# Loading x by halves of the lanes instead of by halves of its rows, in a DMA-fed graph layer on one core

## The chip, the core and the metric

The kernel runs on one core of a Trainium2 chip. The metric is the device time in microseconds (us) of one execution. It was run three times before the change, and once more with the profiler on.

## What is computed

With N = 5000 nodes and F = 64 features, the reference is:

```python
h = jnp.maximum(_layernorm(x, axis=-1), 0.0)
neighbors = adj_matrix @ h                      # 5000 x 5000 by 5000 x 64, float32
neighbors = neighbors / (num_neighbors[:, None] + 1e-07)
out = jnp.concatenate([h, neighbors], axis=-1) @ fc_w.T + fc_b
x = x + jax.nn.relu(out)
```

Nearly all bytes are those of the 5000 x 5000 float32 matrix adj, 100 MB, each of which is read once.

## The kernel before

**Layout.** A core's fast memory has 128 lanes. The first 4,608 nodes of x lie as 36 rows on each of the 128 lanes (lane p holds nodes 36p to 36p + 35), so that one lane's share is 36 x 64 x 4 = 9,216 contiguous bytes in the chip's main memory. The other 392 nodes lie as 4 rows on 98 lanes. adj comes in six column groups; each group is read in loads of up to four row tiles, the largest of which are 5,120 KB, 128 lanes x 40,960 bytes.

**Queues.** All loads of adj (33 of them) are issued by SyncE (SP), in a written order, into a ring in the tile `raw`, which holds three of the largest loads. A load whose place is still in use waits for `load_used`, the semaphore that TensorE raises when it has multiplied the load that lay there. The x of the first 4,608 nodes is loaded by `load_x(engine, k)`, called once on SP's queue with k = 0, ahead of every adj load, and once on ScalarE's (ACT's) queue with k = 1. Behind it ACT's queue issues the layer's weights fc_t (into the tile shown as `rnn_diag`), the bias, and the last 392 nodes of x. In the trace, q1 holds what SP issues and q10 what ACT issues.

**Order of the work.** `normalize(b)` on VectorE (DVE) works on five sets of eight tiles of x and waits first for both halves of x (`x_loaded[0]` at 32, 16 from each half). Its product, `h_pairs`, is transposed by TensorE (`turn`, L589), copied by ScalarE (L360), and multiplied with the weights (`weigh`, L601) into `g_sb`, which needs the weights to have landed and to have been doubled (L695). Only then do the multiplications with adj begin (`multiply`, L641). Sets 1 to 4 are normalized, turned and weighed between the multiplications of the first group. At the end each finished bank is scaled, turned back, and added to x; the result leaves in two stores.

Of the kernel before, what the change touches and what calls it, by code (L numbers as in the profile page):

```python
# [12 lines left out]
LANES = 128  # L13
# [31 lines left out]
def gnn_layer(nc, x, adj_groups, num_neighbors, fc_t, fc_b, out):  # L45
# [16 lines left out]
    TAIL0 = FULL * BLOCK  # L62
    REM0 = CH * LANES
    ROWS = FULL * RUN
# [59 lines left out]
    with ExitStack() as ctx:  # L124
        def sb(name, shape, dt=F32):
            return ctx.enter_context(nc.sbuf_tensor(name, shape, dt))
# [6 lines left out]
        x_sb = sb("x_sb", [LANES, TILES, F])  # L133
# [76 lines left out]
        def flat(v):  # L210
            return v.rearrange("p t f -> p (t f)")
# [41 lines left out]
            return landed[n % LANDINGS], 16 * (n // LANDINGS) + 16  # L253

        def load_x(engine, k):
            r = slice(ROWS // 2 * k, ROWS // 2 * (k + 1))
            engine.dma_start(x_sb[:, r, :], x[0:TAIL0, :].rearrange("(p r) f -> p r f", r=ROWS)[:, r, :]
                             ).then_inc(x_loaded[0], 16)

        def sync_program(sp):  # L260
            def load(n):
                g, m, i0, i1 = LOADS[n]
                w = WIDTH[g]
                if loads_before(n):
                    sp.wait_ge(load_used, loads_before(n))
                r = RUN if m < FULL else TAIL_RUN
                rows = adj_groups[g][m * BLOCK:m * BLOCK + r * LANES, 0:w].rearrange("(p i) c -> p (i c)", i=r)
                sp.dma_start(raw[:, place(n):place_end(n)], rows[:, i0 * w:i1 * w]).then_inc(loaded(n)[0], 16)

            load_x(sp, 0)  # L270
            for n in range(len(LOADS)):
                load(n)

            sp.wait_ge(out_ready, LAST)
            sp.dma_start(out[0:TAIL0, :].rearrange("(p r) f -> p (r f)", r=ROWS), flat(out_sb[:, 0:ROWS, :])
                         ).then_inc(stored, 16)
            sp.wait_ge(stored, 16)
# [40 lines left out]
        def scalar_program(act):  # L318
            def load_few():

                load_x(act, 1)
                act.dma_start(w_rows.rearrange("r (k c) -> r k c", k=2), fc_t.rearrange("(k r) c -> r k c", k=2)
                              ).then_inc(weights_loaded, 16)
                act.wait_ge(bias_cleared, 1)
                act.dma_start(bias_row[0:1, :], fc_b.rearrange("(a f) -> a f", a=1)).then_inc(bias_loaded, 16)
                act.dma_start(tail(x_sb)[0:PAD0], tail_nodes(x)[0:PAD0]).then_inc(x_loaded[1], 16)
                act.wait_ge(x_cleared, 1)
                act.dma_start(tail(x_sb)[PAD0:LAST_LANES], tail_nodes(x)[PAD0:LAST_LANES]).then_inc(x_loaded[1], 16)  # L330
# [431 lines left out]
```

## Time and profile before

| what | us |
|---|---|
| median of three runs | 246.04 |
| lowest, highest | 245.55, 246.4 |
| the profiled execution's own time | 246.15 |
| its span in the profile | 244.7 |
| TensorE (PE) busy | 201.6 |
| VectorE (DVE) busy | 41.7 |
| ScalarE (ACT) busy | 15.8 |

The span covers the program's instructions; 246.15 - 244.7 = 1.45 us of the profiled execution lie around it. The mean granted clock of TensorE was 0.993 of full. In the profile, a packet is one contiguous piece moved by one of the 16 DMA engines, and a share of busy time of "the 16 engines" is a mean over them. A packet is put into the stretch in which it ends, so a short stretch can show a share above 1 or none.

### The profile page before, as it was taken

The numbers are of one execution on the slowest core, as the hardware profiler recorded it, in microseconds if no ns is written. First come the engines' busy times: TensorE is split into PE (matmuls) and PEld (weight loads), VectorE is DVE, ScalarE is ACT, GpSimd is POOL, SyncE is SP. The second block draws the span as 40 slices with busy tenths as digits, with TensorE's granted clock in tenths as the row PEclk, the third lists the DMA queues.
The fourth block names the chain that finished last, engine by engine and source line by source line (L and its number), as shares of the span: only waits on it lengthen the run. The fifth ranks groups of instructions, "written<-read, shape, count | busy, mean of one in ns | idle before, by whom it ended". The sixth has DMA issues, their size and how long they took to land.

```text
span 244.7 us, 2442 instructions
## 1 busy us (share of the span) xinstructions
PE 201.6 (82%) x1090; PEld 85.9 (35%) x1090; DVE 41.7 (17%) x102; ACT 15.8 (6%) x36; POOL 6.1 (2%) x17
## 2 busy tenths in 40 slices
PE   0016899999879987997799897969899687996995
PEld 0014445435323433442343242424244232332354
DVE  1623404314400200050000530203000000000052
ACT  2102121201200110010000300000000000000000
POOL 6000010000000000000010000000000000000000
PEclk9999999999979999999999999999999999999999
DMA  8999999999999999999999999999999999999996
GB/s 300 431 431 438 435 429 410 426 429 429 426 442 442 429 425 429 429 429 408 425 435 428 460 424 434 408 460 424 440 408 459 404 445 399 429 429 412 414 393 254
DMA packets 5983, 102.76 MB, mean 420 GB/s; under 512 B 1122, under 2 KB 1710, under 8 KB 2902
## 3 DMA queue, kind: packets, MB, share of 16 engines
q1 hardware_dynamic: 5040, 101.61, 97.4%
q10 hardware_dynamic: 774, 0.84, 1.0%
q8 instruction: 8, 0.13, 0.2%
q0 software_dynamic: 160, 0.16, 0.2%
q14 instruction: 1, 0.01, 0.0%
HBM read 101.33 MB, written 1.28 MB: 419 GB/s over the span
## 4 chain that ended last, share of the span: by engine, by line
DMA 53%; PE 32%; issue 11%; DVE 2%; ACT 0%; ACTq 0%; DVEq 0%
DMA raw<-adj_group 46%; PE acc L641 24%; DMA rnn_diag<-fc_t 8%; PE turned L641 3%; PE y L601 3%; DVE rnn_diag L487 1%; PE y L626 1%; PE turned L589 0%; PE y L695 0%; PE y L618 0%; ACT g_sb L366 0%; PE y L669 0%; ACT w_both L387 0%; DVE out_sb L550 0%; DVE rnn_diag L495 0%
## 5 line engine op out<-in xcount | busy, mean ns | idle before, releaser
L641 PE MATMUL acc<-raw,g_sb 128*64 128x512 f32 (+1 forms) x780 | 160.3, 557 | 20.3 <-DMA raw<-adj_group 19.6
L641 PEld LDWEIGHTS acc<-raw,g_sb 128*64 128x64 f32 x780 | 55.2, 137 | 107.0 <-issue 75.2
L641 PE MATMUL turned<-raw,g_sb 128*64 128x196 f32 x156 | 18.2, 337 | 0.1
L641 PEld LDWEIGHTS turned<-raw,g_sb 128*64 128x64 f32 x156 | 11.4, 136 | 14.7 <-issue 13.7
L589 PE MATMUL turned<-ident,h_pairs 128*128 128x128 f32 x20 | 3.7, 315 | 12.4 <-DVE h_pairs L446 12.4
L516 DVE TENSOR_TENSOR sums<-acc,rnn_bc 128x512 f32<-128x512 f32 x4 | 2.7, 689 | 64.9 <-PE acc L641 63.0
L458 DVE TENSOR_TENSOR out_sb<-y,bias 128x128 f32<-128x128 f32 x20 | 4.4, 284 | 48.7 <-ACT g_sb L366 48.6
L601 PE MATMUL y<-w_both,ht 128*128 128x256 f32 (+1 forms) x40 | 11.9, 437 | 0.7 <-ACT w_both L387 0.7
L601 PEld LDWEIGHTS y<-w_both,ht 128*128 128x128 f32 x40 | 8.0, 217 | 3.9 <-issue 1.5
L434 DVE TENSOR_REDUCE var<-sums 128x8 f32<-128x512 f32 x5 | 3.4, 686 | 24.2 <-ACT sums L341 24.2
L542 DVE TENSOR_TENSOR out_sb<-y,out_sb 128x512 f32<-128x512 f32 (+1 forms) x5 | 3.2, 636 | 24.8 <-PE y L669 20.9
L589 PEld LDWEIGHTS turned<-ident,h_pairs 128*128 128x128 f32 x20 | 2.4, 156 | 13.9 <-issue 13.9
L366 ACT ACTIVATE g_sb<-y 128x256 f32<-128x256 f32 x10 | 3.3, 381 | 49.3 <-PE y L601 30.8
L695 PE MATMUL y<-rnn_diag,ident 64*64 64x128 f32 x4 | 0.7, 444 | 6.3 <-DMA rnn_diag<-fc_t 6.3
L487 DVE TENSOR_TENSOR rnn_diag<-ident,rnn 128x512 f32<-128x512 f32 x8 | 5.1, 687 | 0.2 <-PE y L626 0.2
L626 PE MATMUL y<-rnn_diag,ones 128*64 128x512 f32 (+1 forms) x20 | 4.6, 552 | 0.5 <-DVE rnn_diag L487 0.4
L371 ACT ACTIVATE rnn_bc<-y 128x512 f32<-128x512 f32 (+1 forms) x5 | 2.9, 588 | 31.7 <-PE y L626 31.7
L492 DVE TENSOR_TENSOR rnn_diag<-ident_twice,rnn 128x256 f32<-128x256 f32 x1 | 0.4, 426 | 25.7 <-issue 25.7
L423 DVE TENSOR_REDUCE mean<-x_sb 128x8 f32<-128x512 f32 (+1 forms) x6 | 3.5, 589 | 5.7 <-DMA x_sb<-x 5.7
L360 ACT ACTIVATE ht<-turned 128x512 f32<-128x512 f32 x5 | 3.0, 597 | 21.0 <-PE turned L589 21.0
L656 PE MATMUL acc<-adj_rem,g_sb 128*64 128x512 f32 (+1 forms) x20 | 4.2, 549 | 0.0
L430 DVE TENSOR_TENSOR cen<-x_sb,mean 128x512 f32<-128x512 f32 (+1 forms) x6 | 3.5, 603 | 0.2
(63 smaller groups left out, 47.2 us busy)
## 6 DMA issues: line engine op xcount, KB each, us to landing
raw<-adj_group SPq DMA_DIRECT2D x9, 5120.0 KB, 25.9
raw<-adj_group SPq DMA_DIRECT2D x6, 4880.0 KB, 24.4
raw<-adj_group SPq DMA_DIRECT2D x4, 2048.0 KB, 21.4
raw<-adj_group SPq DMA_DIRECT2D x1, 4096.0 KB, 24.2
raw<-adj_group SPq DMA_DIRECT2D x1, 3840.0 KB, 24.4
raw<-adj_group SPq DMA_DIRECT2D x2, 1024.0 KB, 23.9
raw<-adj_group SPq DMA_DIRECT2D x4, 392.0 KB, 22.8
out<-out_sb SPq DMA_DIRECT2D x1, 1152.0 KB, 4.4
```

The costliest lines, as they stand in the source:

```text
L366: nc.scalar.activation(to[:, 2 * k:2 * k + 2, :, :], weighed_parts(k, 1), ACT.Copy).then_inc(g_copied, 1)
L423: last = nc.vector.tensor_reduce(narrow(mean[:]), rows, AX_X, ALU.add)
L430: last = nc.vector.tensor_tensor(wide(cen[:]), rows, m.unsqueeze(len(m.shape)).to_broadcast(list(rows.shape)), ALU.subtract)
L434: nc.vector.tensor_reduce(var[:], sums[0][:].rearrange("p (t f) -> p t f", f=F), AX_X, ALU.add).then_inc(ln_dve, 1)
L458: last = nc.vector.tensor_tensor(to[:, 2 * k:2 * k + 2, :], weighed_parts(k, 0)[:, :, s, :], bias[:].unsqueeze(1).to_broadcast([LANES, 2, ...
L487: last = nc.vector.tensor_tensor(split(to[:, s, :]), ident[:].unsqueeze(1).to_broadcast(shape), rnn[:, m + s:ROWS:FULL].unsqueeze(2).to_br ...
L542: nc.vector.tensor_tensor(o, split(y[b % 2][:, 0:RUN * F * (m1 - m0)]), o, ALU.add).then_inc(summed, 1)
L589: last = nc.tensor.transpose(turned[:, c], h_pairs[b % 2][:, c], ident[:])
L601: last = nc.tensor.matmul(weighed_tiles(i)[:, 0:w], ht[b % 2][:, c:c + LANES], flat(w_both[:])[:, 0:w], start=True, stop=True)
L626: last = nc.tensor.matmul(y[b % 2][k, c], ones[:, 0:HALF], r, start=True, stop=True, tile_position=(0, s * HALF))
L641: last = nc.tensor.matmul(acc[b][s * HALF:(s + 1) * HALF, 0:width], g_sb[:, t, :], k, start=t == 0, stop=t == CH - 1, tile_position=(0, s ...
L656: last = nc.tensor.matmul(acc[b][s * HALF:(s + 1) * HALF, 0:width], g_sb[:, CH, :], k, start=False, stop=False, tile_position=(0, s * HALF))
```

## The change

Both `load_x` transfers still carry 576 KB each and are still issued at the same places of the same queues. Before, each took 18 of the 36 rows of all 128 lanes: 128 packets of 4,608 bytes. After, SP's queue takes all 36 rows of lanes 0 to 63 and ACT's queue all 36 rows of lanes 64 to 127: 64 packets of 9,216 bytes each. Nothing else is different.

```diff
         def load_x(engine, k):
-            r = slice(ROWS // 2 * k, ROWS // 2 * (k + 1))
-            engine.dma_start(x_sb[:, r, :], x[0:TAIL0, :].rearrange("(p r) f -> p r f", r=ROWS)[:, r, :]
+            p = slice(k * LANES // 2, (k + 1) * LANES // 2)
+            engine.dma_start(flat(x_sb[p, 0:ROWS, :]), x[0:TAIL0, :].rearrange("(p r) f -> p (r f)", r=ROWS)[p, :]
                              ).then_inc(x_loaded[0], 16)
```

## Rows read from the trace of the kernel before

**Rows 1.** The page: the span in 40 slices, and packets of each queue.
```profile
DMA  8999999999999999999999999999999999999996
GB/s 300 431 431 438 435 429 410 426 429 429 426 442 442 429 425 429 429 429 408 425 435 428 460 424 434 408 460 424 440 408 459 404 445 399 429 429 412 414 393 254
...
q1 hardware_dynamic: 5040, 101.61, 97.4%
q10 hardware_dynamic: 774, 0.84, 1.0%
```

**Rows 2.** Waits: who waited for whom, us in total, times, longest.
```profile
PE acc L641 <- DMA raw<-adj_group: 19.6, 11, 3.1
```

**Rows 3.** The chain that ended last, in order of time: start us, us, what.
```profile
1.20 18.52 DMA rnn_diag<-fc_t
...
19.76 0.71 PE y L695 x4
...
21.18 3.59 PE y L601 x8
...
25.60 8.81 PE acc L641 x48
...
45.86 23.10 DMA raw<-adj_group
...
213.54 21.92 DMA raw<-adj_group
...
237.71 3.99 PE turned L641 x44
```

**Rows 4.** Timeline, 0 to 35 us: start us, us, engine line op.
```profile
0.75 0.38 SPq L257 DMA_DIRECT2D x_sb<-x  x1
0.76 0.40 ACTq L257 DMA_DIRECT2D x_sb<-x  x1
...
7.38 0.69 DVE L423 TENSOR_REDUCE mean<-x_sb 128x8 f32<-128x512 f32 x1 [5.68 <-DMA x_sb<-x]
...
13.52 0.60 ACT L360 ACTIVATE ht<-turned 128x512 f32<-128x512 f32 x1 [2.69 <-PE turned L589]
```

**Rows 5.** Timeline of SP's queue, 24 to 36 us.
```profile
34.45 0.33 SPq L268 DMA_DIRECT2D raw<-adj_group  x1
```

**Rows 6.** DMA issues of x: KB each, us to landing.
```profile
x_sb<-x SPq DMA_DIRECT2D x1, 576.0 KB, 4.9
x_sb<-x ACTq DMA_DIRECT2D x1, 576.0 KB, 6.6
```

**Rows 7.** Stretches of 0.2 us; the last two columns are DMA share and GB/s.
```profile
1.60:1.80 0.20, 0.00 (x0) 0.00 (x0) 0.10 (x2) 0.00 (x0) 0.20 (x2) 1.00 1.58 138
1.80:2.00 0.20, 0.00 (x0) 0.00 (x0) 0.00 (x0) 0.00 (x0) 0.20 (x1) 1.00 1.83 184
2.00:2.20 0.20, 0.00 (x0) 0.00 (x0) 0.00 (x0) 0.00 (x0) 0.20 (x1) 1.00 0.16 23
...
2.40:2.60 0.20, 0.00 (x0) 0.00 (x0) 0.00 (x0) 0.00 (x0) 0.20 (x1) 1.00 0.11 46
2.60:2.80 0.20, 0.00 (x0) 0.00 (x0) 0.00 (x0) 0.00 (x0) 0.20 (x1) 1.00 0.74 276
...
3.60:3.80 0.20, 0.00 (x0) 0.00 (x0) 0.00 (x0) 0.20 (x1) 0.20 (x1) 1.00 1.06 438
```

**Rows 8.** DMA queues in 85 ns: from 3.870, 3.955 and 4.125 us; share of 16 engines.
```profile
q10 hardware_dynamic: 4, 0.02, 52.4%
q1 hardware_dynamic: 1, 0.00, 13.1%
...
q10 hardware_dynamic: 7, 0.03, 91.6%
q1 hardware_dynamic: 3, 0.01, 39.3%
...
q1 hardware_dynamic: 7, 0.03, 91.6%
q10 hardware_dynamic: 3, 0.01, 39.3%
```

**Rows 9.** DMA queues, 12 to 13.5 us: packets, MB, share of 16 engines.
```profile
q1 hardware_dynamic: 16, 0.66, 101.0%
q10 hardware_dynamic: 16, 0.00, 1.2%
```

## The prediction

> **What bounds the kernel now.** I read the page's row of DMA slices first: the 16 engines are busy in 9 tenths or more of every slice but the first and the last, at 400 to 460 GB/s [rows 1]. TensorE has time over: it waits 19.6 us, in 11 places, for adj to land [rows 2]. The chain then says the same in order of time: after the first multiplications it runs over landings of adj, again and again, up to one at 213.54 + 21.92 = 235.46 us, behind which there are only some 6 us of TensorE and the last stores [rows 3]. So the end is set by one stream of packets that has no hole once it runs. Whatever keeps its engines from moving bytes for 1 us moves the last landing, and the end, by 1 us.
>
> The front of the chain needs a second look, since the change is there. It begins with the weights, not with x: they land at 19.72 us, the first set of x is turned and copied at 13.52 + 0.60 = 14.12 us, and the multiplications with adj begin at 25.60 [rows 3, 4]. This head isn't what sets the end either. The ring holds three loads; the fourth is issued at 34.45 us, when the first is used up [rows 5]. The three loads are 24 packets on each engine, and a packet of 40,960 bytes takes 1.0 x 24 / 16 = 1.515 us (101.0% of 16 engines x 1.5 us, for 16 packets) [rows 9], so from about 5.3 us they keep the engines busy until 5.3 + 24 x 1.515 = 41.7 us (SP's half of x lands at 0.75 + 4.9 = 5.65, completion included; 1.1 of the 1.18 MB from 2.6 us on at 438 GB/s end at 5.1 [rows 6, 7]). The fourth comes 7 us before that. Taking some 1 us from an issue to its first bytes off (x: issued at 0.75, first packets ended from 1.6 on [rows 4, 7]), the head could be 6 us later before the stream ran dry.
>
> **What the change adds and removes.**
>
> Packets. The page's 5,040 packets of q1 are 35 transfers (33 of adj, one of x, one store) of 128 + 16 each: eight data packets and one completion on each of the 16 engines [rows 1]. With 64 packets, I take four for each engine and queue; q1 would then have 4,976, q10 710. A packet of 4,608 bytes takes 13.1% of 16 x 0.085 us = 0.178 us [rows 8]. At the rate of the long packet (40,960 / 1.515 = 27.0 GB/s for an engine [rows 9]) its bytes take 0.170, so a packet costs 0.008 us of its own. Each engine has 8 fewer in all: -0.06 us.
>
> The start. The first 14 packets end between 1.60 and 2.00 us ((138 + 184) x 0.2 us / 4.608 KB); then there are 23 to 46 GB/s until 2.60, and only after that the full rate [rows 7]. Whatever makes this hole, each engine goes into it with one packet done. If that one carries 9,216 bytes, 4,608 more are over when the hole ends: -0.17 us. The issues themselves (0.38 and 0.40 us [rows 4]) may become some tens of ns shorter; nothing waits for that, since the queues behind them are fed from far ahead.
>
> The lanes. Here lies the disputed cost. Before, every transfer of x and nearly every other byte goes to all 128 lanes, eight lanes for an engine. No row shows a large transfer to half the lanes, so the cost is bounded from both sides. If the way into the memory's lanes can take what all engines bring, wherever it goes, the cost is 0. If each group of lanes can take only what one engine has been seen to deliver, 27.0 GB/s [rows 9], half the lanes take half the rate: while all engines work on SP's packets (lanes 0 to 63) two engines share each group's way in, and both take twice the time. It doesn't help that ACT's packets go to the other half if the engines take turns in step. And they mostly do: at 3.955 us seven packets of q10 end and three of q1, and at 4.125, half a turn later, seven of q1 and three of q10 [rows 8]. About 7 in 10 are in step. The price at worst: a packet of 9,216 bytes takes 0.34 us at 27.0 GB/s, and 0.34 more where the way is shared. An engine has 8 such packets. The first falls before the hole: it would end at about 1.9 + 0.17 + 0.34 = 2.4 us, about when the next ones start to end (2.4 to 2.6 [rows 7]), so it costs next to nothing. Seven are left: 7 x 0.34 = +2.4 us. Two engines that start apart share the way for less: the second packets end within some 0.3 us (12 of them in 2.60 to 2.80 [rows 7]), so a pair is on average 0.1 us apart and shares that much less of each turn, 7 x 0.1 = 0.7 us. But a load counts as landed when its slowest engine is done, and that belongs to a pair that is close together; I take half, -0.35.
>
> [...]
>
> The sum: 2.4 - 0.35 - 0.17 - 0.06 = +1.8 us. I take the upper side of the disputed cost because the trace shows the engines in step, and both bounds stay for the range: with 0 in place of 2.05 the sum is -0.23.
>
> **What hides and what doesn't.** x lands some 1.8 us later (now at 5.65 and, ACT's half, at 0.76 + 6.6 = 7.36 [rows 4, 6]), the first reduce of DVE moves from 7.38 [rows 4] to about 9.2, and the copy of the first turned set from 14.12 to 15.9. Behind x on ACT's queue stand the weights, eight packets for each engine that alternate with long adj packets of 1.5 us; they move with the end of x, from 19.72 to about 21.5, and so does the first multiplication, from 25.60 to 27.4. The set of x is still ready 5.6 us before the weights. The fourth load would be issued at 36.3, with the stream's own end of supply moved to 43.5: covered as before. If that cover were gone each us of the head would count, but it isn't near. So nothing is added for the head, and nothing subtracted: the stream is late by 1.8 us itself. 246.15 + 1.8 = 247.95 for the profiled execution; it stood 0.1 above the median, so I say 247.8.
>
> **Rivals.**
>
> The transfer to half the lanes costs nothing, or the engines get out of step at once. For it: 3 in 10 packets are out of step now [rows 8], a pair in opposite turns never shares, and packets may queue ahead of the way in so that it stays full. Against: 9,216 bytes is a longer turn than 4,608, so the same difference in start gives less relief. Time: 246.04 - 0.23 = 245.8, no measurable change. 0.34.
>
> The halves are written one after the other in full. The whole 1,152 KB at half of 438 GB/s [rows 7] takes 5.4 instead of 2.7 us, +2.7, and the first packets aren't covered by the hole: 248.7. Against it stands that two queues are served at once [rows 8]. 0.13.
>
> On the other side: the hole from 2.0 to 2.6 us belongs to the making of the packet lists, which are half as long now. If it shrinks by its whole 0.5 us and the lanes cost nothing, the sum is -0.5 - 0.23 = -0.73, 245.3, just over 0.3% faster. It decides from the point at which the second packets end before about 2.1 us. Against: no issue's duration follows its number of packets in a plain way, and the rate after the hole is full, so the lists weren't what was slow then. 0.07.
>
> **How the numbers follow.** My forecast has 0.46. 0.3% of 246.04, about what a measurement of this kernel can tell from no change, is 0.74 us. Slower by more: 0.46 + 0.13, less 0.05 for pairs so far apart that under 0.74 us is left: 0.54. Within: 0.34 + 0.05, less 0.01: 0.38. Faster: 0.07 + 0.01 = 0.08. The range reaches down to the case of no cost, with the runs' own spread of 0.4 us around it, 245.5, and up to the full double time with some 0.3 us of spread, 249.0. Since cases of both signs of "costs something" hold much, the likeliest one's own range is 246.9 to 248.6.
>
> **What the profile after would show.** First the packets: 64 of 9,216 bytes in each queue, 4,976 in q1. If half the lanes are half as fast, the rate from 2.6 us on stays well under 438 GB/s, a packet of 9,216 bytes takes up to 0.68 us instead of 0.35, and the first reduce of DVE starts at about 9.2; the last landing of adj is 1.8 us later and the steady part is as long as before. If x costs nothing, a packet takes 0.35 us, the reduce starts at 7.2 to 7.4 and the end stays. I would be wrong if the first landings came late but the last ones didn't, so that something later in the stream gives the time back; or if the time changed while x landed as before, which would make the order in which engines go on from x the cause, and not the lanes.

## The result, and the profile after

The change made the kernel slower: 248.52 us (248.18 to 248.76, six runs) against 246.2 us (245.55 to 246.4, six runs) before. The ratio is 1.0098, with a 95% interval of 1.0088 to 1.0108, that is 2.2 to 2.7 us more. 247.8 was forecast, with a range of 245.5 to 249.0 and slower as the likeliest. The profiled execution took 248.65 us with a span of 247.2, 2.5 us more than before on both counts.

The page's slices and queues after, to be read beside [rows 1]: from the third slice on the rates are those of before, and the loss is in the first two, 158 and 352 GB/s in place of 300 and 431. (158 - 300 + 352 - 431) x 6.2 us is 1.4 MB, a good 3 us at the full rate; part of it is packets that begin a little later, across a slice's edge. The packets are 64 fewer in each queue.

```profile
DMA  6999999999999999999999999999999999999996
GB/s 158 352 434 423 435 426 428 432 425 424 441 437 444 451 444 420 424 424 424 404 438 438 434 445 417 449 442 407 436 430 449 408 429 411 429 427 419 412 394 262
...
q1 hardware_dynamic: 4976, 101.61, 96.8%
q10 hardware_dynamic: 710, 0.84, 1.5%
```

One reading made ahead of the result has to be set right first. A packet is counted in the stretch in which it begins, not in which it ends. In the kernel before, the packets of x alone fill the 16 engines until 5.4 us (in the 0.34 us from 4.38 us those of q1 take 52.4% of the engines' time and those of q10 49.1%). The first 16 packets of adj, 1.51 us each, are counted from 5.2 to 5.6 us, the next 16 from 6.7 to 7.1; had the first ones ended there, they would have been under way beside x from 3.7 to 4.1 us on. The prediction's hole from 2.0 to 2.6 us is therefore no pause: in it the first packets are under way, 0.78 us each:

```profile
q1 hardware_dynamic: 14, 0.06, 194.9%
```

(the kernel before, 1.70 to 2.05 us; 1.949 x 16 x 0.35 us / 14 = 0.78 us). Averages over 16 packets below, one for each engine, are taken from the single packets of the trace in the order in which they begin.

The DMA queues of the changed kernel in single stretches of 0.34 us, from 2.68, 3.02, 4.04, 6.42 and 7.44 us (packets, MB, share of 16 engines), to be read beside [rows 8]:

```profile
q1 hardware_dynamic: 13, 0.12, 96.3%
...
q1 hardware_dynamic: 12, 0.11, 138.5%
...
q1 hardware_dynamic: 8, 0.07, 109.0%
...
q10 hardware_dynamic: 8, 0.07, 107.9%
...
q1 hardware_dynamic: 9, 0.37, 313.7%
q10 hardware_dynamic: 4, 0.00, 1.4%
```

From 3.4 us on about eight packets of 9,216 bytes begin in each 0.34 us, 217 GB/s. One takes 109.0% of 16 x 0.34 us / 8 = 0.74 us; two packets of 4,608 took 2 x 0.178 = 0.36. All of q1's x comes first and then all of q10's; the two queues no longer alternate. The last two lines hold nine of the first 16 adj packets behind x: 3.137 x 5.44 us / 9 = 1.9 us for one, where 1.515 is usual [rows 9]. (A share above 100% in a short stretch is the time of packets that begin in it and run on beyond it.)

The head, in the timeline of the changed kernel, beside [rows 3, 4]; the last line is SP's queue at the fourth load, beside [rows 5]:

```profile
0.75 0.54 SPq L257 DMA_DIRECT2D x_sb<-x  x1
0.76 0.56 ACTq L257 DMA_DIRECT2D x_sb<-x  x1
...
10.09 0.69 DVE L423 TENSOR_REDUCE mean<-x_sb 128x8 f32<-128x512 f32 x1 [8.39 <-DMA x_sb<-x]
...
16.23 0.60 ACT L360 ACTIVATE ht<-turned 128x512 f32<-128x512 f32 x1 [2.69 <-PE turned L589]
...
22.42 0.69 PE L695 MATMUL y<-rnn_diag,ident 64*64 64x128 f32 x4 [6.23 <-DMA rnn_diag<-fc_t]
...
36.94 0.33 SPq L268 DMA_DIRECT2D raw<-adj_group  x1
```

And its chain of waits, beside [rows 3]:

```profile
1.36 21.02 DMA rnn_diag<-fc_t
...
28.10 8.81 PE acc L641 x48
...
216.08 21.89 DMA raw<-adj_group
```

The first reduce is 2.71 us later, the weights (22.38) 2.66, the first multiplication 2.50, the fourth load 2.49, and the last awaited landing of adj (216.08 + 21.89 = 237.97, before 235.46) 2.51. The time is lost by about 9.5 us and never comes back.

### The profile page after: what moved, and what is told of

Same layout as the page of the kernel before. It is cut to its first block, busy times and chain, and to the rows that moved or that the text cites. A ratio compares the mean times of both kernels' runs of the same rounds, so it can differ in the third digit from the quotient of the medians.

```text
span 247.2 us, 2442 instructions
## 1 busy us (share of the span) xinstructions
PE 201.6 (82%) x1090; PEld 85.8 (35%) x1090; DVE 41.7 (17%) x102; ACT 15.8 (6%) x36; POOL 6.1 (2%) x17
## 3 DMA queue, kind: packets, MB, share of 16 engines
q1 hardware_dynamic: 4976, 101.61, 96.8%
## 4 chain that ended last, share of the span: by engine, by line
DMA 55%; PE 31%; issue 11%; DVE 2%; ACT 0%; ACTq 0%; DVEq 0%
DMA raw<-adj_group 46%; PE acc L641 23%; DMA rnn_diag<-fc_t 9%; PE turned L641 3%; PE y L601 2%; DVE rnn_diag L487 1%; PE turned L589 1%; PE y L626 1%; PE y L695 0%; PE y L618 0%; ACT g_sb L366 0%; PE y L669 0%; ACTq L257 0%; ACT w_both L387 0%; DVE rnn_diag L495 0%
## 5 line engine op out<-in xcount | busy, mean ns | idle before, releaser
L458 DVE TENSOR_TENSOR out_sb<-y,bias 128x128 f32<-128x128 f32 x20 | 4.4, 283 | 49.1 <-ACT g_sb L366 49.0
L341 ACT ACTIVATE sums<-cen 128x512 f32<-128x512 f32 x5 | 3.1, 627 | 6.8 <-DVE cen L430 6.5
```

Source lines behind the costliest of these rows:

```text
L341: nc.scalar.activation(sums[0][:], cen[:], ACT.Square).then_inc(ln_act, 1)
L458: last = nc.vector.tensor_tensor(to[:, 2 * k:2 * k + 2, :], weighed_parts(k, 0)[:, :, s, :], bias[:].unsqueeze(1).to_broadcast([LANES, 2, ...
```

## The experiments

Three theories. Theory 1: half the lanes take half the rate, and the stream of packets loses that time. Theory 2: the packets do it, fewer and longer ones for each engine. Theory 3: the later head does it. All times are medians; each set of runs had its own runs of the kernel before, with medians from 246.05 to 246.10. Where an edit adds a transfer, the wait for its landing counts 16 more for each; those lines aren't shown.

**Short packets, first attempt.**

```diff
-            engine.dma_start(flat(x_sb[p, 0:ROWS, :]), ...[p, :]
+            to = x_sb[p, 0:ROWS, :].rearrange("p (h r) f -> p h (r f)", h=2)
+            rows = x[0:TAIL0, :].rearrange("(p h r) f -> p h (r f)", h=2, r=ROWS // 2)
+            engine.dma_start(to, rows[p]).then_inc(x_loaded[0], 16)
```

> Halves of the lanes as in the change, but each lane's 9,216 bytes in two packets of 4,608, so 128 packets in a queue as before. Theory 1 (the lanes: 64 lanes take half the rate, whatever the packets): as slow as the change, about 248.5 us, x of both queues through at about 7.2 us, the first reduce of DVE after 9.5 us; whether or not the two queues take turns. Theory 2 (the packets: four long ones for each engine and queue instead of eight short ones make the queues go one after the other and leave engines idle): like before, about 246.2 us, the first reduce at about 7.4 us.

248.3 us, ratio 1.0094 (1.0079 to 1.0110). But q1 has 4,976 packets, as in the change: the two pieces of a lane lie next to each other in both memories and went as one packet. This is the change once more and says nothing about theory 2; the repeat is further down.

**One transfer of all lanes.**

```diff
-            p = slice(k * LANES // 2, (k + 1) * LANES // 2)
-            engine.dma_start(flat(x_sb[p, 0:ROWS, :]), ...[p, :]
+            engine.dma_start(flat(x_sb[:, 0:ROWS, :]), x[0:TAIL0, :].rearrange("(p r) f -> p (r f)", r=ROWS)
-                load_x(act, 1)
-                dve.wait_ge(x_loaded[0], 32)
+                dve.wait_ge(x_loaded[0], 16)
```

> All of x (36 rows of 128 lanes, 128 packets of 9,216 bytes) in one transfer on SP's queue; DVE waits for that one alone. Theory 1 (the lanes): full rate, x through at about 5 us, the time 0.1 to 0.3 us under before, 245.9 to 246.1. Theory 2 (long packets are what costs): still slow, 247.5 or more. Theory 3 (what costs is the later head: the weights and the first multiplication): the weights land earlier or as before, so like before too.

246.19 us, ratio 1.0007 (0.9999 to 1.0016). Packets of 9,216 bytes cost nothing by themselves. The first reduce starts at 5.96 us, 1.4 us before that of the kernel before, and that is worth nothing either. The gain of 0.1 to 0.3 us that I expected isn't there: the first adj packets begin at 5.45 us on average, where they begin at 5.40 in the kernel before.

**Both halves on SP's queue.**

```diff
             load_x(sp, 0)
+            load_x(sp, 1)
-                load_x(act, 1)
```

> The change, but both halves of the lanes are issued on SP's queue, one behind the other. Theory 1 in the form that the trace of the change suggests (each engine works through one queue's transfer before the other's, with all engines on the same half of the lanes): nothing is lost by it, about 248.5 us, x through at about 7.2 us. If the two queues did overlap in part in the change, this one is slower by that part, up to 0.5 us.

248.59 us, ratio 1.0100 (1.0086 to 1.0114): the same as the change. The weights now have ACT's queue to themselves, and the head is early, earlier even than before:

```profile
21.44 2.80 PE L641 MATMUL acc<-raw,g_sb 128*64 128x512 f32 x14 [0.83 <-DMA raw<-adj_group]
```

The first multiplication with adj starts at 21.44 us in place of 28.10, and the kernel is as slow. That speaks against theory 3.

**A later head, with no byte changed.**

```diff
+            dve.wait_ge(x_loaded[0], 32)
+            rows, narrow, wide = parts(0)[0]
+            for i in range(12):
+                nc.vector.tensor_reduce(narrow(mean[:]), rows, AX_X, ALU.add).then_inc(late, 1)
+                dve.wait_ge(late, i + 1)
             normalize(0)
```

> The kernel before, with 12 needless reductions (of 0.69 us) on DVE before the first set of x is normalized; no byte and no packet is different. They make the first multiplication with adj some 2.5 to 3 us later, as in the change. Theory 1 (the stream of packets lost 2.4 us): the time stays at 246.2. Theory 3 (the later head costs): about 248.5 us.

246.0 us, ratio 0.9996 (0.9988 to 1.0005). Its timeline shows that the first multiplication was indeed as late as in the change:

```profile
28.22 4.09 PE L647 MATMUL acc<-raw,g_sb 128*64 128x512 f32 x20 [0.52 <-ACT g_sb L367]
```

Theory 3 has fallen: the ring covered a head 2.6 us late in full.

**A load of adj by halves of the lanes,** nine times the bytes of a half of x.

```diff
-                sp.dma_start(raw[:, place(n):place_end(n)], rows[:, i0 * w:i1 * w]).then_inc(loaded(n)[0], 16)
+                cuts = [(0, HALF), (HALF, LANES)] if n == 1 else [(0, LANES)]
+                for p0, p1 in cuts:
+                    sp.dma_start(raw[p0:p1, place(n):place_end(n)], rows[p0:p1, i0 * w:i1 * w]
+                                 ).then_inc(loaded(n)[0], 16)
```

> The kernel before, with the second load of adj (5,120 KB, packets of 40,960 bytes) issued as two transfers, lanes 0 to 63 and then lanes 64 to 127. Theory 1 (64 lanes take half the rate, for any packet and in the steady stream): this load takes 24.2 instead of 12.1 us and the kernel about 258 us. Theory 2 (the loss belongs to the start, to x or to short packets): no more than 0.5 us, 246 to 247.

259.48 us, ratio 1.0544 (1.0528 to 1.0559), 13.4 us more; 12.1 were expected for the load. In its stretches of 6 us (the last two columns are DMA share and GB/s) the engines are busy all the time, at half the rate while the halves of the lanes are written, and at the full one later. The page's slices of 6.4 us show 207 to 211 GB/s inside the load, and a packet takes 3.0 to 3.2 us there; the 219 below is one stretch:

```profile
30.00:36.00 6.00, 6.00 (x36) 2.75 (x34) 0.00 (x0) 0.00 (x0) 0.00 (x0) 1.00 1.04 219
...
48.00:54.00 6.00, 6.00 (x34) 2.97 (x32) 0.96 (x5) 0.66 (x2) 0.00 (x0) 1.00 1.04 437
```

**The control: the same load in two transfers of all lanes** (`cuts` of columns, `[(0, 2 * w), (2 * w, 4 * w)]`, in place of lanes).

> The control to the split by lanes: the same load as two transfers of 128 lanes with packets of 20,480 bytes. Both theories: no change, 246.2 us within 0.3, since one transfer more costs only its packets (8 more for an engine, 0.008 us each).

246.18 us, ratio 1.0003 (0.9994 to 1.0012). The number of transfers isn't it.

**x by even and odd lanes.**

```diff
-            p = slice(k * LANES // 2, (k + 1) * LANES // 2)
+            p = slice(k, LANES, 2)
```

> The change with other lanes: SP's queue takes the even lanes and ACT's the odd ones, 64 packets of 9,216 bytes each. If it matters that a transfer covers only half of the range of lanes: like before, 246.0 to 246.3. If it matters which engines write to which lanes at the same time (two engines in step on the same group): still slow, between 247 and 248.5. If any transfer of 64 packets is slow: 248.5.

246.41 us, ratio 1.0014 (1.0005 to 1.0023). The transfers have the change's very packets, 64 of 9,216 bytes in each queue (4,976 and 710 packets), and even its order, q1's x before q10's; only the lanes are others. Between 4.72 and 5.06 us:

```profile
q10 hardware_dynamic: 16, 0.15, 103.9%
```

Sixteen packets in 0.34 us where the change has eight, 1.039 x 5.44 / 16 = 0.35 us for one in place of 0.74. This is the cleanest pair of the study. The 0.3 us that are left over are just clear of zero, and the trace shows where they arise: the first packet of x begins at 2.08 us as in the change, not at 1.76 as before, and the first adj packets begin 0.31 us later than before (5.70 on average, before 5.40) and take the usual 1.51 us. So some 0.3 us of the change's loss belong to transfers of 64 lanes as such, and not to which lanes they are.

**x by quarters of the lanes** (four transfers of 32 lanes, two on each queue: `p = slice(q * LANES // 4, (q + 1) * LANES // 4)`).

> x in four transfers of 32 lanes and 32 packets each, 0 to 31 and 32 to 63 on SP's queue, 64 to 95 and 96 to 127 on ACT's. If the rate falls with the number of lanes (32 lanes a quarter of the rate): x takes some 10.8 us and the kernel 254 or more. If 32 lanes reach as much of the memory as 64 do (lanes 0 to 31 and 32 to 63 share the same ways in): like the change, 248.5 us within 0.5.

247.85 us, ratio 1.0065 (1.0048 to 1.0082), +1.8: not four times as slow, and a little better than halves: the first packet begins at 1.77 us, and the first adj packets at 7.00 on average, where those of the change begin at 7.49. Here two queues did take turns at first: in the stretch from 3.02 to 3.36 us they began 14 packets, 379 GB/s:

```profile
q1 hardware_dynamic: 6, 0.06, 60.6%
q10 hardware_dynamic: 8, 0.07, 52.9%
```

**Short packets, again,** with transfers of 18 rows that can't be joined.

```diff
+            for h in range(2):
+                r = slice(ROWS // 2 * h, ROWS // 2 * (h + 1))
+                engine.dma_start(x_sb[p, r, :], x[0:TAIL0, :].rearrange("(p r) f -> p r f", r=ROWS)[p, r, :]
+                                 ).then_inc(x_loaded[0], 16)
```

> Halves of the lanes as in the change, but each queue loads its half in two transfers of 18 rows, so that its packets really have 4,608 bytes (the earlier edit left 64 packets of 9,216 bytes in a queue, since a lane's two pieces lie next to each other on both sides; it repeated the change). Theory 1 (the lanes alone): 248.0 to 248.6 us, and 5,056 packets in q1. Theory 2 (long packets, or four of them for an engine): 246.2.

248.46 us, ratio 1.0101 (1.0084 to 1.0118), with the expected 5,056 packets in q1. With 4,608 bytes to a packet as before, on half the lanes as in the change, it is the change's time. Theory 2 has fallen from both sides: long packets to all lanes are fast (one transfer), short ones to half the lanes are slow.

**Which lanes? A load of adj cut at lanes 32 and 96** (`cuts` of `slice(32, 96)`, `slice(0, 32)`, `slice(96, LANES)`).

> The second load of adj in three transfers on SP's queue: lanes 32 to 95, lanes 0 to 31, lanes 96 to 127. If the number of lanes of a transfer sets its rate (64 lanes half, 32 lanes half or less): at least 12 us more, 258 us or over. If what counts is how much of 0 to 63 and of 64 to 127 a transfer reaches: the 64 lanes in the middle go at the full rate (6 us), the two of 32 lanes, each in one half only, at half rate (6 us each), together 18 instead of 12 us: about 252 us.

252.75 us, ratio 1.0286 (1.0265 to 1.0308), +6.65. Its stretches of 6 us show the middle lanes go by at the full rate (a packet takes 1.54 to 1.57 us, round by round), and then the two outer quarters at half rate (2.94 to 3.20 us), some 12 us long:

```profile
18.00:24.00 6.00, 3.26 (x10) 2.39 (x11) 1.59 (x4) 1.38 (x4) 0.00 (x0) 1.00 1.01 385
24.00:30.00 6.00, 5.36 (x27) 2.83 (x28) 3.15 (x10) 0.66 (x2) 0.00 (x0) 1.00 0.90 190
30.00:36.00 6.00, 5.45 (x34) 2.61 (x30) 0.00 (x0) 0.51 (x1) 0.00 (x0) 1.00 0.98 206
```

So here 64 lanes, half of them on each side of lane 64, were as good as 128, and 32 lanes within one side as good as 64 there (2.88 to 3.20 us for a packet in the load cut at lane 64).

**The same with even and odd lanes** (`cuts` of `slice(0, LANES, 2)` and `slice(1, LANES, 2)`).

> The second load of adj in two transfers of 64 lanes, the even ones and then the odd ones. If 64 lanes are slow as such: 259.5 us as with the halves. If a transfer is slow only where it stays within 0 to 63 or 64 to 127: 246.2 to 246.6 us.

246.15 us, ratio 1.0004 (0.9995 to 1.0014): no cost at all on 5.24 MB.

**The halves of a load on two queues,** the third load, lanes 0 to 63 on SP's queue and 64 to 127 on ACT's.

```diff
+                p = slice(HALF, LANES)
+                act.dma_start(raw[p, place(2):place_end(2)], rows[p, i0 * w:i1 * w]).then_inc(loaded(2)[0], 16)
...
+                p = slice(0, HALF) if n == 2 else slice(0, LANES)
+                sp.dma_start(raw[p, place(n):place_end(n)], rows[p, i0 * w:i1 * w]).then_inc(loaded(n)[0], 16)
```

> The third load of adj by halves of the lanes, lanes 0 to 63 on SP's queue and 64 to 127 on ACT's, issued at the start and so both waiting while the first two loads run. If two queues with the two halves serve each other, as they did not in the change: near before, 246.5 us. If the engines take turns in step: as slow as both halves on one queue, about 259 us. In between if only some engines are out of step. The weights lie ahead of it on ACT's queue, so the head is as before.

259.32 us, ratio 1.0544 (1.0515 to 1.0573), as slow as both halves on one queue. The queues of this kernel from 38.0 to 40.8 and from 40.8 to 43.6 us:

```profile
q1 hardware_dynamic: 9, 0.37, 59.9%
q10 hardware_dynamic: 7, 0.29, 46.6%
...
q10 hardware_dynamic: 9, 0.37, 59.8%
q1 hardware_dynamic: 7, 0.29, 46.5%
```

In each stretch 16 packets begin, one for each engine, and in either round about half of them go to lanes 0 to 63 and the other half to lanes 64 to 127. Yet a packet takes 0.599 x 44.8 us / 9 = 3.0 us and not 1.5. The two queues do alternate here, and it doesn't help. (A round really takes as long as its packets, 3.0 us: from one to the next the mean start moves from 39.07 to 42.04 us, 220 GB/s.)

## Why the prediction was right, and where it was off

**The bound.** One stream of packets sets the end: right. In the split loads and the change the time moved by about what the stream lost, and neither the late head (246.0) nor the early ones (one transfer 246.19, both halves on SP 248.59) moved it at all.

**What is hidden.** The head's cover was priced at 6 us; the run with the late head used 2.6 of them at no cost. In the change the weights were 2.66 us later and not 1.8, with the stream, as described.

**Packets.** 4,976 and 710: exact. The credits for them were -0.06 and -0.17 us; the whole x in one transfer has the same long packets on all lanes and should show both, and is no faster than before (ratio 0.9999 to 1.0016). In its trace some 0.2 us are saved between the first packets of x and the first of adj (3.29 us, before 3.50), but the first packets begin 0.26 us later on average (2.16 and 1.90). So neither can be counted on.

**The start.** There is no hole that could cover anything; the first packets fill it. What the prediction concluded from it holds all the same: the first packet cost nothing for its lanes (0.62 us for 9,216 bytes, where even and odd lanes took 0.91 and the kernel before 0.76 for 4,608). But the transfers themselves start later, which the prediction ruled out: it expected the issues to become some tens of ns shorter. They took 0.54 and 0.56 us in place of 0.38 and 0.40, the first packet of x began at 2.08 us in place of 1.76, and the first 16 began 0.41 us later on average (2.30 and 1.90).

**The lanes.** I took the right side of the bound, and this term came out as forecast. The seven later packets of an engine took 4.63 us in the change and 2.48 with even and odd lanes, whose packets are the same: +2.15, against 2.4 - 0.35 = +2.05. The relief for engines that start apart lies mostly at the start: 13 and 12 packets begin in the two stretches from 2.68 to 3.36 us where the later pace would have been eight each; 9 more are 9 / 8 x 0.34 = 0.38 us.

**What x cost in all, and what came behind it.** The first 16 packets of adj begin at 5.40 us on average before and at 7.49 after: +2.10, where the sum said +1.8. The rest of the loss falls in these packets themselves. The lines are the kernel before from 6.7 to 7.2 us (a usual round of adj), and the change from 7.1 to 7.9 us (its first round) and from 9.2 to 9.7 us (its second):

```profile
q1 hardware_dynamic: 16, 0.66, 302.8%
...
q1 hardware_dynamic: 16, 0.66, 244.0%
...
q1 hardware_dynamic: 16, 0.66, 305.7%
```

One packet takes 3.028 x 8.0 us / 16 = 1.51, 2.440 x 12.8 / 16 = 1.95 and 3.057 x 8.0 / 16 = 1.53 us. In the kernel before the first round took 1.51 like every other. So the first round behind x costs 0.44 us more, and the second begins 2.53 us later than before (9.45 and 6.92 on average); the last landing is 2.51 later.

So the sum failed in two steps, though the forecast held. It gave the start a credit of 0.17 us and no delay, where the first packets began 0.41 us later, and it took the disputed cost to be over when x is through, where the next round of packets still pays 0.44 us. In figures, 0.41 for the later start, 1.69 from the first packets of x to the first of adj, and 0.44 in the first round of adj make 2.54 us. Why the first round is slow no run shows: its packets begin from 7.19 to 7.83 us, while packets of x to lanes 64 to 127 are under way until 7.84; behind even and odd lanes, where adj begins from 5.40 to 6.00 us and x is under way until 6.00 too, it takes 1.51. The split load of adj shows the same: its first full round takes 1.95 us too, and 0.5 of its 13.4 us arise there; the load itself cost 12.8 in place of 12.1.

**The reason given for the double time** was that the engines take turns between the queues in step. It doesn't hold as stated. In the change there were no turns (q1's x went first, as in the rival that priced a full one-after-the-other at 248.7, and the measured 248.52 lies nearer to that rival's number than to mine, in part by luck: it has neither the late start nor the slow first round). In the run with short packets the queues took turns by whole transfers, and with adj on two queues by single packets, with about half the engines on either side; both were as slow. So the order of the queues isn't the cause at all. That two engines share a way into the lanes was the prediction's own assumption, and no view here shows it; nor does a run show what else makes such a transfer slow. What the runs do show is the rate by lanes: 207 to 217 GB/s on one side of lane 64 (the split load's slices, x in the change) against some 430 on both, 32 lanes of one side no slower than 64, the middle 64 lanes at the full rate, and no gain from the other side on a second queue (259.32 us, on one queue 259.48).

**The other rivals.** No cost for half the lanes: refuted at 13.4 us on one load. A start that becomes quicker with shorter packet lists: refuted, the start became slower, as said above.

No version here beats the kernel before. Of the ways to cut x, the one by rows, the one transfer and the even and odd lanes are within 0.3 us of each other, and only those that keep each transfer within lanes 0 to 63 or 64 to 127 are slower.

## What to carry to other kernels

Where the DMA engines set the end, as here, cut a transfer by rows (246.2 us) or columns (246.18), or into interleaved lanes (246.15 for a load of adj, 246.41 for x), and not at lane 64: in these runs a transfer that stayed on one side of it took about twice the time per byte (2.9 to 3.2 us for a packet of 40,960 bytes of the split load in place of 1.5), and a second queue with the other side didn't give it back (259.32 us, 259.48 on one queue). Look at the rate in the stretch where the transfer runs, not at the engines' busy share, which was 1.04 at 219 GB/s as at 437. And before moving work in the head of a kernel, ask whether it or the stream behind it sets the end: 2.6 us of delay cost nothing here, and the same delay in the stream cost all of it.

## What the runs showed of the hardware that I had not expected

- Queues that both held work didn't always alternate packet by packet: with 64 packets in a queue, nearly all of q1's x began before q10's first at the full rate (even and odd lanes) as all of it did at half rate (the change), where transfers of 128 packets alternated. The quarters, transfers of 32 packets, alternated in blocks: 16 of q1, 16 of q10, the same again, then 32 and 32. What decides between these orders, no run shows.
- With eight engines or so on each side of lane 64 at a time, the sixteen still moved only 220 GB/s (16 packets of 40,960 bytes in 3.0 us).
- A transfer written with two pieces to a lane went as one packet of 9,216 bytes where the pieces are neighbours in both memories. The packet count in the profile is the way to see whether such an edit took effect.
- As the first x transfer on its queue, one to 64 contiguous or alternate lanes took 0.54 to 0.59 us to issue, one to 128 lanes 0.36 to 0.41, though the first had half the packets; two to 32 lanes took 0.85 and 0.89 together. Where the first transfer went to 64 lanes its first packet began at 2.08 or 2.09 us, where it went to 128 or 32 at 1.75 to 1.77.
- The first full-width packets behind a transfer that stayed on one side of lane 64 were slow too: 1.95 us in place of 1.51, behind x as behind the split load.
